# State-space layer: three float32r passes in place of one float32 product, two passes moved to ScalarE, down weights loaded late

## The reference

```python
xz = x @ W_in                                   # 256 -> 2 x 512
xc, z = jnp.split(xz, 2, axis=-1)
xt = conv(xc, conv_w)                           # causal, 4 taps for each channel
u = silu(xt)
dt_raw, B_raw = jnp.split(u @ W_x, 2, axis=-1)
dt = clip(softplus(dt_raw @ W_dt + b_dt), 1e-4, 1.0)
ub = u * (B_raw @ W_Bp)
h = h * (1.0 - dt_t) + ub_t                     # scan over 512 tokens
y = (h + D_param * u) * silu(z);  out = y @ W_out
# experts, over the same normalised rows
router = xf @ Wg;  top_logits, idx = top_k(router, 2);  probs = softmax(top_logits)
y  = sum over the 2 chosen of 8: probs * ((silu(xf @ W1[e]) * (xf @ W2[e])) @ W3[e])
y += (silu(xf @ Ws1) * (xf @ Ws2)) @ Ws3        # shared experts, 2 x 352 wide, every row
```

## Time and profile before

| | |
|---|---|
| three runs | 3282.55, 3285.95, 3296.76 us (median 3285.95) |
| span of the profiled execution | 3217.5 us |
| median less span (start and end around the instructions) | 68.45 us |
| TensorE busy | 2948.1 us, 92% |
| VectorE / ScalarE / GpSimd busy | 58% / 41% / 10% |
| mean granted TensorE clock | 0.953 |
| state-space layer, first XC to last OUT | 1661.4 to 2174.1 us |

### The profile page before, as it was taken

The page is one execution under the profiler, slowest core; times in us unless marked ns, Lnnn a source line. Parts: engine busy times, 40 slices in busy tenths (PEclk is TensorE's granted clock), DMA queues, the critical chain, the costliest instruction groups (busy, mean ns, idle before and its releaser), DMA issues.

```text
span 3217.5 us, 50027 instructions
## 1 busy us (share of the span) xinstructions
PE 2948.1 (92%) x14054; PEld 1750.6 (54%) x14087; DVE 1872.7 (58%) x4526; ACT 1332.2 (41%) x1921; POOL 313.0 (10%) x349
## 2 busy tenths in 40 slices
PE   5999999999989888888899999999999599999998
PEld 3455545554544444444445565556666366666666
DVE  5656665656637777777746776772222455555552
ACT  1544453445334555554553433422233144444443
POOL 0000000000000000000001111221111311111110
PEclk7999999999987999999998999999999699999999
DMA  6433543454222112121331110112221443334340
GB/s 210 138 102 90 158 131 98 108 151 138 72 67 62 58 61 67 59 62 55 101 135 68 42 52 33 46 46 71 103 64 59 103 97 93 93 93 93 93 92 16
DMA packets 144298, 279.77 MB, mean 87 GB/s; under 512 B 22384, under 2 KB 80112, under 8 KB 134160
## 3 DMA queue, kind: packets, MB, share of 16 engines
q1 hardware_dynamic: 131760, 244.90, 26.5%
q0 software_dynamic: 10464, 28.59, 3.2%
q10 hardware_dynamic: 2016, 5.58, 0.5%
HBM read 179.31 MB, written 99.68 MB: 87 GB/s over the span
## 4 chain that ended last, share of the span: by engine, by line
PE 77%; DVE 9%; DMA 5%; issue 4%; ACT 3%; SPq 1%; DVEq 0%; POOL 0%; ACTq 0%; POOLq 0%
PE bank L488 8%; PE bank_u L559 6%; PE pair L599 5%; PE pair L543 5%; PE pair L700 4%; PE pair L1984 4%; PE bank_m L488 3%; DVE nmax L870 3%; PE pair L2819 3%; PE bank_m L2783 3%; PE pair L744 3%; PE bank L2783 3%; PE pair L2434 3%; PE bank L520 2%; PE pair L499 2%
## 5 line engine op out<-in xcount | busy, mean ns | idle before, releaser
L776 ACT ACTIVATE probs<-pair 128x1024 f32<-128x1024 f32 x512 | 501.4, 1021 | 215.4 <-PE pair L543 214.4
L870 DVE TENSOR_REDUCE nmax<-bank 128x1 f32<-128x512 f32 x664 | 441.7, 685 | 212.0 <-PE bank L520 149.3
L870 DVE TENSOR_REDUCE nmax<-bank_m 128x1 f32<-128x512 f32 x360 | 246.4, 684 | 112.1 <-PE bank_m L520 67.4
L559 PE MATMUL bank_u<-probs,vext 128*32 128x512 f32 x2048 | 296.0, 652 | 0.6 <-ACT uraw L763 0.5
L520 PE MATMUL bank<-k_a,q_a 96*128 96x512 f32 x336 | 173.2, 550 | 22.2 <-DMA k_a<-parts_dram 18.5
L543 PE MATMUL pair<-q_a,k_a 98*128 98x512 f32 x512 | 170.9, 440 | 17.8 <-ACT probs L776 12.4
L2116 DVE CUSTOM_DVE_ANT_0 bank<-bank,mask_q 128x128 f32<-128x128 f32 (+1 forms) x320 | 118.3, 416 | 76.9 <-PE bank L1888 76.1
L543 PEld LDWEIGHTS pair<-q_a,k_a 98*128 98x128 f32 x512 | 88.4, 197 | 114.1 <-ACT probs L776 68.9
L2019 ACT ACTIVATE probs<-pair 128x896 f32<-128x896 f32 x128 | 115.2, 919 | 72.0 <-PE pair L1906 72.0
L1379 PE MATMUL bank<-k,q 62*128 62x512 f32 x302 | 115.1, 484 | 26.5 <-DVE nmax L870 26.5
L1984 PE MATMUL pair<-fc,hid 128*128 128x256 f32 x512 | 131.2, 382 | 6.0 <-ACT probs L2019 6.0
(11 more groups left out here) (391 smaller groups left out, 5752.7 us busy)
## 6 DMA issues: line engine op xcount, KB each, us to landing
parts_dram<-parts SPq DMA_DIRECT2D x64, 512.0 KB, 2.8
q_a<-parts_dram SPq DMA_DIRECT2D x31, 512.0 KB, 6.1
k_a<-parts_dram SPq DMA_DIRECT2D x31, 512.0 KB, 8.1
q<-parts_dram SPq DMA_DIRECT2D x97, 128.0 KB, 2.5
xs<-xres SPq DMA_DIRECT2D x24, 512.0 KB, 3.0
xl<-xs SPq DMA_DIRECT2D x24, 512.0 KB, 3.9
x_in<-xg SPq DMA_DIRECT2D x74, 128.0 KB, 2.0
yg_dram<-y_out POOLq DMA_DIRECT2D x72, 128.0 KB, 2.0
```

The source lines that it names most:

```text
L559: ins = nc.tensor.matmul(bank_u[32 * h:32 * h + 32, :], vext[:, kt, kv(g, h), :], probs[:, kt % 2, h * SEQ:(h + 1) * SEQ], start=(kt == 0) ...
L776: nc.scalar.activation(probs[:, kt % 2, hp * 2 * SEQ:hp * 2 * SEQ + n], st.tile(l, name)[:, 0:n], ACT.Exp).then_inc(st.free["act"].sem, 1)
L870: nc.vector.tensor_reduce(nmax[:, g % 2, qt, h:h + 1], sc.tile(l, name)[:], AX, ALU.max, negate=True).then_inc(sc.free["dve"].sem, 1)
```

## The change

1. **Products.** XC, Z and the shared experts' A and B are no longer float32 matmuls. Rows and weights are held in two parts each, `x_high` and `x_low`, `win_high` and `win_low`, `ab_high` and `ab_low`; the high part is the value rounded to float32r, the low part the rest. `pe_project_split` makes three float32r passes over both halves of the features: high by high, low weight by high row, high weight by low row. That is six matmuls of 512 columns in place of two float32 ones. R, XP and the rest are as before, so `xnT` stays.
2. **Rows.** ScalarE copies T twice (`x_high`, then `xnT`), VectorE makes `x_low` by a subtraction behind its last scan (in the first round behind its setup); the third pass of XC 0 waits for it.
3. **Weights.** GpSimd splits `win` and `sh_ab` once, at the end of its work for the layer before. `win` is now the last but one of the loads.
4. **First tap** of the convolution: from VectorE to ScalarE, behind each copy of XC.
5. **1 - dt**: from VectorE to ScalarE, behind the logarithms; VectorE then limits 1 - dt to between 0 and 1 - 1e-4 in one pass.
6. **Memory and down weights.** The parts need room: `hm` is kept for one expert only, and `moe_c` lies where the state-space layer's tensors were, so it is loaded in LAST2, when the last B is done.

The diff, cut to its core:

```diff
-STEPS_DVE = [(3, 10), (14, 19), {MAIN2: 55, LAST2: 69}, {PRE3: 6, MAIN3: 25, POST3: 6}, {COMB: 13}]
+STEPS_DVE = [(3, 10), (14, 19), {MAIN2: 47, LAST2: 61}, {PRE3: 6, MAIN3: 25, POST3: 6}, {COMB: 13}]
...
+            sp.dma_start(win[:], d["win"]).then_inc(win_loaded, 16)
             sp.dma_start(sh_ab[:], d["sh_ab"]).then_inc(shared_loaded, 16)
...
+            sp.wait_ge(weights_split, 4)
             sp.dma_start(sh_c[:], d["sh_c"]).then_inc(loaded2b, 16)
             sp.dma_start(wout[:], d["wout"]).then_inc(loaded2b, 16)
             for e in range(EXPERTS):
                 sp.dma_start(moe_ab[:, e], d["moe_ab"][:, e]).then_inc(loaded2c, 16)
-                sp.dma_start(moe_c[:, e], d["moe_c"][:, e]).then_inc(loaded2c, 16)
...
+        def pe_project_split(pe, l, it, name, high, low, at, n=P, first=False):
+
+            for s in s2.vacated(l, it, name):
+                pe.wait_ge(*s)
+            for j, (w, x) in enumerate(((high, x_high), (low, x_high), (high, x_low))):
+                if first and j == 2:
+                    pe.wait_ge(*x_split.at(l, it))
+                for k in range(KT):
+                    ins = nc.tensor.matmul(s2.tile(l, name)[0:n, :], w[:, k, at:at + n].bitcast(F32R), x[:, k, :].bitcast(F32R),
+                                           start=(j == 0 and k == 0), stop=(j == 2 and k == KT - 1))
+            ins.then_inc(s2.full.sem, 1)
...
             for c in range(CT):
-                pe_project(pe, l, it, ("XC", c), win, c, ring=s2)
+                pe_project_split(pe, l, it, ("XC", c), win_high, win_low, c * P, first=(c == 0))
...
-                pe_project(pe, l, it, ("Z", c), win, CT + c, ring=s2)
+                pe_project_split(pe, l, it, ("Z", c), win_high, win_low, (CT + c) * P)
...
-                    pe_project(pe, l, it, ("A", e, i), sh_ab[:, e], 0, n, None, at, s2)
-                    pe_project(pe, l, it, ("B", e, i), sh_ab[:, e], 0, n, None, 352 + at, s2)
+                    pe_project_split(pe, l, it, ("A", e, i), ab_high[:, e], ab_low[:, e], at, n)
+                    pe_project_split(pe, l, it, ("B", e, i), ab_high[:, e], ab_low[:, e], 352 + at, n)
...
+        def act_copy_split(act, l, it):
+
+            act.wait_ge(*st.filled(l, it, "T"))
+            flat = st.tile(l, "T")[:]
+            nc.scalar.activation(x_high[:, :, :].rearrange("p k n -> p (k n)").bitcast(F32R), flat, ACT.Copy)
+            nc.scalar.activation(xnT[:, :, :].rearrange("p k n -> p (k n)"), flat, ACT.Copy).then_inc(st.free["act"].sem, 1)
...
+            def first_tap(c):
+                act.wait_ge(*done(s2, l, it, ("XC", c)))
+                nc.scalar.activation(cv[:, c, :], xc[:, c, 0:SEQ], ACT.Identity, scale=conv[:, c, 0:1]).then_inc(tap_ready.sem, 1)
...
+            def keep(c):
+                step.wait(CT + c + 1)
+                nc.scalar.activation(dtb[:, c, :], dtb[:, c, :], ACT.Identity, bias=1.0, scale=-1.0).then_inc(dt_ready.sem, 1)
...
             for c in range(CT):
                 step.wait(c + 1)
-                nc.scalar.activation(dtb[:, c, :], dtb[:, c, :], ACT.Ln, bias=1.0).then_inc(dt_ready.sem, 1)
+                step.mark(nc.scalar.activation(dtb[:, c, :], dtb[:, c, :], ACT.Ln, bias=1.0))
+                if c:
+                    keep(c - 1)
+            keep(CT - 1)
...
+        def dve_split_x(dve, l, it):
+
+            dve.wait_ge(*done(st, l, it, "T"))
+            fence(dve)
+            nc.vector.tensor_tensor(x_low[:, :, :].rearrange("p k n -> p (k n)").bitcast(F32R), st.tile(l, "T")[:],
+                                    x_high[:, :, :].rearrange("p k n -> p (k n)"), ALU.subtract).then_inc(x_split.sem, 1)
...
             def convolve(c):
-                dve.wait_ge(*done(s2, l, it, ("XC", c)))
-                step.mark(nc.vector.tensor_scalar(cv[:, c, :], xc[:, c, 0:SEQ], conv[:, c, 0:1], None, ALU.mult))
+                dve.wait_ge(*tap_ready.at(l, it, c + 1))
...
-                step.mark(nc.vector.tensor_scalar(dtb[:, c, :], dtb[:, c, :], 1e-4, 1.0, ALU.max, ALU.min))
-                step.wait()
-                step.mark(nc.vector.tensor_scalar(dtb[:, c, :], dtb[:, c, :], -1.0, 1.0, ALU.mult, ALU.add))
+                step.mark(nc.vector.tensor_scalar(dtb[:, c, :], dtb[:, c, :], 0.0, 1.0 - 1e-4, ALU.max, ALU.min))
...
+        def pool_split_weights(pool):
+            pool.wait_ge(win_loaded, 16)
+            nc.gpsimd.tensor_copy(win_high[:].bitcast(F32R), win[:]).then_inc(weights_split, 1)
+            pool.wait_ge(shared_loaded, 16)
+            nc.gpsimd.tensor_copy(ab_high[:].bitcast(F32R), sh_ab[:]).then_inc(weights_split, 1)
+            pool.wait_ge(weights_split, 2)
+            nc.gpsimd.tensor_tensor(win_low[:].bitcast(F32R), win[:], win_high[:], ALU.subtract).then_inc(weights_split, 1)
+            nc.gpsimd.tensor_tensor(ab_low[:].bitcast(F32R), sh_ab[:], ab_high[:], ALU.subtract).then_inc(weights_split, 1)
...
             if l == LAST2:
+                sp.wait_ge(*s2.filled(l, it, ("B", 1, 2)))
+                for e in range(EXPERTS):
+                    sp.dma_start(moe_c[:, e], d["moe_c"][:, e]).then_inc(loaded2c, 16)
                 sp_blocks_begin(sp)
```

More of the change, by code:

```diff
@@ L2259, in build @@
         moe_ab = sb("moe_ab", [P, EXPERTS, KT, 704], F32, l2)
-        moe_c = sb("moe_c", [P, EXPERTS, 3, DIM], F32, l2)
         ones_p = sb("ones_p", [P, P], F32, l2)
@@ L2286, in build @@
         wx = sb("wx", [P, CT, 112], F32, mamba)
-        spare2 = sb("spare2", [P, 12], F32, mamba)
+        spare2 = sb("spare2", [P, 8], F32, mamba)
+        win_high = sb("win_high", [P, KT, 1024], F32, mamba)
+        win_low = sb("win_low", [P, KT, 1024], F32, mamba)
+        x_high = sb("x_high", [P, KT, SEQ], F32, mamba)
+        x_low = sb("x_low", [P, KT, SEQ], F32, mamba)
+        ab_high = sb("ab_high", [P, 2, KT, 704], F32, mamba)
+        ab_low = sb("ab_low", [P, 2, KT, 704], F32, mamba)
         low_rows = sb("low_rows", [P, 2], F32, mamba)
-        win = sb("win", [P, KT, 1024], F32, mamba)
-        sh_ab = sb("sh_ab", [P, 2, KT, 704], F32, mamba)
         conv = sb("conv", [P, CT, 4], F32, mamba)
@@ L2299, in build @@
         before = sb("before", [P, P], F32, mamba)
+        whole = ExitStack()
+        win = sb("win", [P, KT, 1024], F32, whole)
+        whole.close()
         wout = sb("wout", [P, CT, DIM], F32, mamba)
@@ L2306, in build @@
         dtb = sb("dtb", [P, CT, SEQ], F32, mamba)
+        spare3 = sb("spare3", [P, 1880], F32, whole)
+        sh_ab = sb("sh_ab", [P, 2, KT, 704], F32, whole)
+        whole.close()
         ub = sb("ub", [P, CT, SEQ], F32, mamba)
         sil = sb("sil", [P, 2, SEQ], F32, mamba)
-        hm = sb("hm", [P, 2, 3, SEQ], F32, mamba)
+        hm = sb("hm", [P, 3, SEQ], F32, mamba)
         mamba.close()
+        moe_c = sb("moe_c", [P, EXPERTS, 3, DIM], F32, l2)
         x_in = sb("x_in", [P, 2, DIM], F32, l2)
@@ L2330, in build @@
         N_SET2 = 14
-        shared_loaded = sem("shared_loaded")
+        win_loaded, shared_loaded = sem("win_loaded"), sem("shared_loaded")
+        weights_split = sem("weights_split")
         spare_cleared = sem("spare_cleared")
@@ L2336, in in_mamba @@
             return [0, 0, {MAIN2: n, LAST2: n}, 0]
+        x_split = sig("x_split", [0, 0, {PRE2: 1, MAIN2: 1}, 0], "vector")
+        tap_ready = sig("tap_ready", in_mamba(CT), "scalar")
         cv_ready = sig("cv_ready", in_mamba(CT), "vector")
@@ L2433, in expert_out @@
                     for i, (at, n) in enumerate(HT):
-                        nc.tensor.matmul(st.tile(l, "OUT")[:, t * DIM:(t + 1) * DIM], hm[0:n, e, i, t * P:(t + 1) * P],
+                        nc.tensor.matmul(st.tile(l, "OUT")[:, t * DIM:(t + 1) * DIM], hm[0:n, i, t * P:(t + 1) * P],
                                          sh_c[0:n, e, i, :], start=(e == 0 and i == 0 and t % 2 == 0), stop=False)
-            pe.wait_ge(shared_loaded, 16)
             expert_in(0)
@@ L2521, in convolve @@
             def convolve(c):
-                dve.wait_ge(*done(s2, l, it, ("XC", c)))
-                step.mark(nc.vector.tensor_scalar(cv[:, c, :], xc[:, c, 0:SEQ], conv[:, c, 0:1], None, ALU.mult))
+                dve.wait_ge(*tap_ready.at(l, it, c + 1))
                 for j in range(1, 4):
-                    step.wait()
+                    if j > 1:
+                        step.wait()
                     ins = nc.vector.scalar_tensor_tensor(cv[:, c, :], xc[:, c, j:j + SEQ], conv[:, c, j:j + 1], cv[:, c, :],
@@ L2702, in dve2 @@
             scan(3)
+            if FRONT[l]:
+                dve_split_x(dve, l, it)
             dve.wait_ge(*st.filled(l, it, "OUT"))
@@ L2959, in _ @@
             pool1(pool, POST1, 0, step)
+            pool_split_weights(pool)
             pool.wait_ge(loaded2, N2)
@@ L2992, in _ @@
             act1(act, POST1, 0, step)
-            act_copy_xnT(act, PRE2, 0)
+            act_copy_split(act, PRE2, 0)
             act.wait_ge(dve_set2, N_SET2)
+            act.wait_ge(weights_split, 4)
```

(2 more changed lines are left out.)

9 lines of the change are left out of this document (5 added, 4 removed).

## The result

| | before | changed |
|---|---|---|
| five runs each, median | 3288.32 us | 3265.14 us (3260.01 to 3270.95) |
| ratio, 95% interval | | 0.9907 [0.9887, 0.9928] |
| predicted | 3285.95 | 3254 (3234 to 3275), ratio 0.9903 |

The account below looks back on a forecast made before the run. TensorE was taken to bound the state-space layer, busy 61.17 of 61.42 us in a steady sequence. Terms of -13.2, -12.6 and -6.0 made -31.8 against 3285.95: 3254 us, range 3234 to 3275.

Parts of the forecast that it names:

- six steady sequences: Middle sequences of the state-space layer: each -4.8 in front, +1.1 behind, +1.5 for slow clock; -13.2 us for six.
- first sequence, T copies included: Layer's first sequence: the wait for xp and its half clock go as down weights leave the queue; -12.6 us.
- last sequence: Layer's last sequence: VectorE gets to hm sooner and product B runs faster; -6.0 us, late down weights costing nothing.
- state-space layer: Sum over the layer's eight sequences: -31.8 us.
- The pass: One 128-row float32r pass on TensorE takes 0.23 us, so a product of three saves 0.17.
- front of a sequence: Projections up to XP, 28 products: 4.8 us less on TensorE, with no new wait.
- The costly pass: Rival: a 128-row float32r pass on TensorE costs 0.34 us, hiding no weight load; +42 us, 3328; chance 0.06.
- The back: After XP: four 1 - dt passes delay ScalarE's sil 2.1 us; TensorE waits 3.5, reaching its transposes 1.1 later.
- The longer tail: Rival: ScalarE's new passes don't overlap, eight taking 5.6 us instead of 4.3; 3263 to 3274; chance 0.19.
- The clock: TensorE runs a short piece at half clock behind each new wait, costing 1.5 us a sequence (0 to 3.4).
- The rest: No new front wait; GpSimd's splits, first tap, x_low and late down weights cost nothing, the last with little to spare.
- the frame: Base of the sum: 3217.5 us of profiled span plus 68.45 around it, together the median of 3285.95.

Follow-up runs that it names:

- e9: The changed kernel, unchanged, run again beside the kernel before in a later series: 3189.87 us against 3217.61, ratio 0.9914.
- e0: The kernel before, unchanged, profiled a second time: 3288.87 us, span 3287.2.
- e1: The changed kernel with 1 - dt back on VectorE, all else as changed: 3244.07 us, ratio 0.986 to the kernel before.
- e6: The changed kernel with 1 - dt and the first tap both back on VectorE: 3168.09 us, ratio 0.9851 to the kernel before.
- e8: The kernel before with only the first tap and 1 - dt moved to ScalarE, float32 products and early weights kept: 3233.53 us, ratio 1.005.
- e3: The kernel before with only the experts' down weights loaded late, at the end of the last sequence: 3282.85 us, ratio 0.9968.

## Why the prediction was right

The prediction is taken here by its own terms, in us. "Prompt" sets e9 against the first profile of before, "late" sets the first profile of the changed kernel against e0.

| term | predicted | prompt | late |
|---|---|---|---|
| six steady sequences | -13.2 | -13.4 (368.56 to 355.16) | -15.5 (384.46 to 368.97) |
| first sequence, T copies included | -12.6 | -13.8 (75.38 to 60.68, copies +0.9) | -10.5 (74.51 to 63.00, +1.0) |
| last sequence | -6.0 | -5.0 (68.76 to 63.71) | -5.4 (67.80 to 62.43) |
| state-space layer | -31.8 | -32.2 | -31.4 |

The last sequence is taken to the transposes of the first block's rows, so it holds what the late down weights cost. That the prompt sum comes within half a us is in part luck: the first sequence gave 1.2 more than predicted and the last 1.0 less.

- *The pass*: 0.227 (six in 1.36 us), predicted 0.23. The front of a sequence is 21.68 instead of 26.27: -4.6 of the 4.8. The costly pass, the only rival that made the kernel slower, is out. The Trainium skill, "TensorE: Matmul & The Clock Gate" (The mechanism, and LDWEIGHTS), by whose rule a pass would take 0.32 in the prediction's estimate, is contradicted for 128 rows too, now that a trace shows them.
- *The back*: predicted 3.5 us of wait, measured 3.26 to 3.27; A10 to A12 grew by 2.09 (6.98 to 9.07). e1, e6 and e8 each show it: A12 starts 2.1 us earlier without the four passes, and 2.1 later with them on the old products. The longer tail did not come; eight passes take 4.28.
- *The clock*: predicted 1.5 a sequence. In e9's six, A12 to T took 2.85 twice, 4.30 twice, 5.23 twice, behind the same wait: 1.3 more than full clock on average. The size held, the picture of "a short one behind each" did not.
- *The rest*: TensorE has no new wait in front, and the splits, the first tap and x_low cost nothing. The down weights were not quite free where signals were prompt: TensorE waits 1.2 us for the first x_in in e9, where the profile before shows no wait; in the first profile of the changed kernel there is none either.

Wrong was the frame. The sum was made "against 3217.5 of span and 68.45 around it": there are 1.7 around it, and the trace on which each term rests shows prompt signals, the times late ones. That it did no harm was luck: the late signal takes its share from both kernels: it puts A12 off by 2.3 us on average in e0 (A10 to A12 9.31 instead of 6.98) and by 1.4 in the changed kernel (10.44 instead of 9.07), where the eight passes stand in the same chain. Had the change taken that place off the path, the terms would not have carried over: in e1, with less in front of A12, the late signal costs a steady sequence 1.6 us (58.15 against 56.57), and in the kernel before 2.65 (64.08 against 61.43).

Of the layer's 31 to 32 us the spans show only 26.3 (prompt) and 23.5 (late). In both pairs the changed profile comes to its last transposes before the layer 8 to 10 us later, in code that the change hardly touches; over 14 profiles these stand at 1654 to 1667 us, on average 1660.7 in kernels with the old layer and 1661.7 in those with the new. That looks like scatter of single executions. For the whole kernel the measures stay apart: 31 us by the ratio and 23 between the medians in the first result, 28 by both in e9. Only the layer's own sum matches the 31.8 closely.

What the prediction missed is that the change holds its own brake: 1 - dt on ScalarE costs 2.6 us in each steady sequence where signals are prompt (59.19 against 56.57) and 3.35 where they are late (61.50 against 58.15), 0.5 to 0.6% of the whole, in exchange for VectorE time that nobody waits for. The prediction had the pieces (2.1 us and a slow stretch) and added them to the back's sum, but never as a part with its own sign.

## What to carry to other kernels

Price each part of a change by itself and give each a sign: here two parts gain (float32r products, late weights), one costs (1 - dt on ScalarE), one does nothing. Before moving a pass, ask who waits for the engine that gets it; ScalarE's share of busy time (38%) said it was free, its place in the chain exp, log, sil said it was not. And check that span and run time agree in one execution of a kernel before building on a profile: 68 us "around the span", where the changed kernel has 1.7, was a sign that profile and times were of different conditions.

## What the runs showed of the hardware

- A signal from TensorE to another engine can arrive long after its product. Against the prompt case it was 0.2 to 3.1 us late at one place of this layer, in sequences 2 to 7, and 7.1 us at one place of the last layer, where the counter was read. It was so in the profile of the first result and in the four of e0 to e3, in both kernels, and in none of the other nine. The kernel before takes 3218 us without it and 3290 with it.
- The same wait of 3.3 us left the granted clock at 1.00 in two sequences of six, and brought it down for part or all of the next 12 products in the other four.
- Float32r passes of 128 rows with new weights each follow one another every 0.227 us at full clock, and every 0.44 at half (12 of them from 1896.79 to 1902.02).
- GpSimd rounds 128x2048 numbers to float32r in 1.89 us and subtracts as many in 4.52. The 2.34 for 128x1024 of the earlier trace rows fits the subtraction; the rounding takes less than half of it.
